# Rows of both attention lanes laid out by dimension in DRAM, and each half of the stacks read back by three transfers

## The reference

```python
x = x + attn_a(layernorm(x))   # memory attention + causal linear attention, 16 heads of 16
x = x + ffn(layernorm(x))      # ternary weights, 256 -> 1024 -> 256, relu
x = x + attn_b(layernorm(x))   # rotary, causal softmax attention, 16 heads of 16
x = x + ffn(layernorm(x))      # the same ffn
```

## Time and profile before

| what | value |
|---|---|
| time, median of 3 runs | 2299.41 us (2298.86 to 2301.97) |
| the profiled execution | 2303.04 us, span 2301.3 us |
| PE (matmul) busy | 1904.0 us, 83% of the span |
| DVE busy | 1617.6 us, 70% |
| ACT busy | 1361.3 us, 59% |
| POOL busy | 1140.6 us, 50% |
| SP's queue: bytes and share of 16 DMA engines | 115.10 MB, 19.8% |
| mean granted TensorE clock | 0.936 |

### The profile page before, as it was taken

How to read it: one execution, slowest core, us unless ns; L and a number is a source line. 1 busy time by engine, 2 the same in 40 slices (tenths; PEclk the granted TensorE clock), 3 DMA queues, 4 the chain that set the end, 5 groups by cost and what they waited for, 6 DMA issues and landing times. The chain is left out here.

```text
span 2301.3 us, 53268 instructions
## 1 busy us (share of the span) xinstructions
PE 1904.0 (83%) x18306; PEld 1207.5 (52%) x18306; DVE 1617.6 (70%) x3890; ACT 1361.3 (59%) x2694; POOL 1140.6 (50%) x978
## 2 busy tenths in 40 slices
PE   0447798989899898989889898989889898988786
PEld 0224455655555555555555555655555555555443
DVE  5546686968777786968777786968777786966351
ACT  0215375666667575666667575666667575665554
POOL 0236347364655547364655547364655547363322
PEclk9757799999999999999999999999999999999998
DMA  3101312304031322303032221304032221303020
GB/s 104 55 10 55 65 57 47 84 5 99 30 70 60 66 66 47 84 9 95 29 70 61 66 66 47 84 2 102 30 65 66 66 66 47 84 2 66 9 58 10
DMA packets 101756, 126.64 MB, mean 55 GB/s; under 512 B 19760, under 2 KB 88496, under 8 KB 97456
## 3 DMA queue, kind: packets, MB, share of 16 engines
q1 hardware_dynamic: 93104, 115.10, 19.8%
q10 hardware_dynamic: 8448, 8.39, 1.1%
HBM read 80.95 MB, written 42.47 MB: 54 GB/s over the span
## 5 line engine op out<-in xcount | busy, mean ns | idle before, releaser
L1268 DVE TENSOR_REDUCE mxs<-bank 128x1 f32<-128x128 f32 (+3 forms) x1024 | 428.0, 482 | 79.7 <-PE bank L1561 78.8
L907 ACT ACTIVATE place<-bank 128x512 f32<-128x512 f32 (+1 forms) x768 | 349.7, 532 | 104.4 <-PE bank L1575 103.1
L669 POOL TENSOR_TENSOR place<-am,place 128x512 f16<-128x512 f32 x256 | 291.0, 1157 | 203.2 <-ACT place L813 203.2
L659 POOL TENSOR_TENSOR place<-place 128x512 f16<-128x512 f32 x256 | 300.7, 1182 | 69.6 <-ACT place L801 64.0
L1559 PE MATMUL bank<-kst,qst 96*128 96x128 f16 (+3 forms) x1024 | 250.8, 306 | 33.5 <-DVE mxs L1268 16.9
L1420 PE MATMUL bank<-w2q,place 128*128 128x256 f16 x2048 | 248.2, 274 | 5.8 <-ACT place L798 4.2
L644 POOL TENSOR_TENSOR rstd<-ve,halfc 128x4 f32<-128x4 f32 x64 | 64.8, 1012 | 364.6 <-DVE ve L1043 364.6
L1573 PE MATMUL bank<-qst,kst 128*128 128x512 f16 (+3 forms) x1024 | 230.7, 302 | 14.6 <-DVE mxs L1268 6.5
L697 POOL TENSOR_TENSOR place<-place 128x512 f16<-128x512 f32 x64 | 83.1, 1301 | 280.9 <-ACT place L837 259.8
L1561 PE MATMUL bank<-mask_qk,identb 128*128 128x128 bf16 x1024 | 218.2, 222 | 0.0
L1420 PEld LDWEIGHTS bank<-w2q,place 128*128 128x128 f16 x2048 | 195.3, 98 | 40.8 <-ACT place L798 11.7
(11 more groups left out here) (162 smaller groups left out, 4134.9 us busy)
## 6 DMA issues: line engine op xcount, KB each, us to landing
by_head<-place SPq DMA_DIRECT2D x64, 256.0 KB, 2.3
qst<-by_head SPq DMA_DIRECT2D x256, 64.0 KB, 2.3
kst<-by_head SPq DMA_DIRECT2D x256, 64.0 KB, 2.3
by_dim<-place SPq DMA_DIRECT2D x64, 256.0 KB, 2.5
kst<-by_dim SPq DMA_DIRECT2D x64, 256.0 KB, 4.7
qst<-by_dim SPq DMA_DIRECT2D x128, 128.0 KB, 5.5
xa<-x SPq DMA_DIRECT2D x16, 512.0 KB, 4.0
out<-xg ACTq DMA_DIRECT2D x16, 512.0 KB, 3.4
```

Of the source, the lines that this page charges most:

```text
L659: G.tensor_tensor(L.hl[:, m, :], L.hf[:, m % 2, :], L.hh[:, m, :], ALU.subtract).then_inc(s["hl"], 1)
L669: G.tensor_tensor(alp[:, n % 2, k, :], am[:, k, :], ahp[:, n % 2, k, :], ALU.subtract).then_inc(s["al"], 1)
L907: A.activation(pf[h % SLOTS][:, S2_COL[k]:S2_COL[k] + S2_W[k]], bank_of(L2, ("S2", h, k))[:, 0:S2_W[k]], ACT.Exp, scale=D ** -0.5 / RS ** ...
L1268: V.tensor_reduce(mxs[:, g:g + 1], bank_of(L2, ("S1", n, k))[:, Q_AT[i]:Q_AT[i] + (i + 1) * P], AX, ALU.max).then_inc(s["mx"], 1)
```

## The change

What a row of the stacks holds is put in another order, so that a whole half can be written to and read from DRAM with few transfers.

- In both lanes the DRAM buffer is now laid out by dimension, then part (high, low), then head. L2's rows already lay by dimension; for L1 the columns of the weights of q and k are permuted at setup (`split_by_dim`), so that row `64r + 4d + i` of a quarter is dimension d of head `4r + i`.
- Each quarter's high and low part is bounced by itself, 128 KB, as soon as it is there: four bounces a half instead of two.
- Each half is read by three transfers: `kst`'s even partitions (high parts, 256 KB), its odd partitions (low parts, 256 KB), and `qst` (512 KB). Each source row is read twice, to two neighbouring partitions, by a repeat of stride 0 that stands second, behind a dimension of 16 rows or more. The bytes are the same as before, 1 MB a half. L1's rows are 4 KB, L2's 8 KB.
- At setup, DVE splits attn_a's q and k weights in 8 strided instructions of 256 elements a partition; `split_by_parity` handles q and k together, with the same 32 instructions of 64 elements as before; the mask that was built on GpSimd (`bd8`) is one reduction on DVE (`bd4`). The chain grows from 66 to 75 links. The 16 small loads of the memories write 16 partitions at a step of 4.
- TensorE's last 16 matmuls of a tile read the same number of columns from other places.

```diff
+                dims, rows = (by_row, P) if L is L1 else (by_dim, PARTS)
+                for which in range(2):
+                    at = 2 * half + which
+                    for part, (name, src) in enumerate((("sh", L.sth), ("sl", L.stl))):
+                        sp.wait_ge(s[name], due(L, name, t, at + 1))
+                        sp.dma_start(dims[half, which, :, part], src[:, at, :]).then_inc(s["bounced"], 16)
+
+                sp.wait_ge(s["bounced"], due(L, "bounced", t, 64 * (half + 1)))
+                stacks = L.qst.shape[1] // KH
+                of_half = slice(half * stacks, (half + 1) * stacks)
+                q_rows = dims[half, 0].rearrange("d a h s -> (d a) (h s)").rearrange("r (o f) -> r o f", o=1)
+                for part in range(2):
+                    k_rows = dims[half, 1, :, part].rearrange("(d o) h s -> d o (h s)", o=1)
+                    sp.dma_start(L.kst[part:rows:2, of_half, :].rearrange("p h s -> p (h s)"),
+                                 k_rows.broadcast_to([rows // 4, 2, stacks * S])).then_inc(L.landed[half], 16)
+                sp.dma_start(L.qst[0:rows, of_half, :].rearrange("p h s -> p (h s)"),
+                             q_rows.broadcast_to([rows // 2, 2, stacks * S])).then_inc(L.landed[half], 16)
...
+            def split_by_dim(mat):
+                stage = w_stage[mat // BQ][:, 0:2 * KH * H].rearrange("p (j i d) -> p j d i", i=QH, d=D)
+                hi, lo = (both(w, mat).rearrange("p (j d i) -> p j d i", i=QH, d=D) for w in (wh, wl))
+                for i in range(QH):
+                    link(V.tensor_scalar(hi[:, :, :, i], stage[:, :, :, i], WS, None, ALU.mult))
+                    link(V.scalar_tensor_tensor(lo[:, :, :, i], stage[:, :, :, i], WS, hi[:, :, :, i],
+                                                ALU.mult, ALU.subtract))
...
-            split_weights(0, BQ)
+            split_by_dim(AQ)
+            split_weights(AV, BQ - AV)
             split_by_parity(BQ)
-            split_by_parity(BK)
...
+            link(V.tensor_reduce(bd4, ident[:, :].rearrange("p (j i) -> p i j", i=QH), AX, ALU.add))
...
-                        ins = T.matmul(local[r][:, i], part[:, n % 2, h % 2, (h // 2) * P:(h // 2 + 1) * P],
+                        ins = T.matmul(local[r][:, i], part[:, n % 2, r, i * P:(i + 1) * P],
```

More of the change, by code:

```diff
@@ L56 @@
 NORM = dict(bn=4, tick=1, mv=4, ve=1, rstd=1, shift=1, xn=4, xt=2, xh=2, xl=2)
-OUTS = dict(v=2, vh=2, sh=4, sl=4, bounced=64, wo=2, xres=2)
+OUTS = dict(v=2, vh=2, sh=4, sl=4, bounced=128, wo=2, xres=2)
 FFN = dict(up=8, hf=8, hh=8, hl=8, xb=1, dn=2, xffn=2)
@@ L69 @@
 PERF = dict(NORM, **FFN, store=16)
-LANDED = {1: 2 * 4 * 2 * 16, 2: 6 * 16}
+LANDED = {1: 3 * 16, 2: 3 * 16}
 CUT = 7
@@ L440, in build @@
         coef = sb("coef", [P, 2, 2, TERMS, QH])
-        bd8 = am[:, 0, 0:HH8]
+        bd4 = am[:, 0, 0:QH]
         t6 = L1.place3[:, 0:3, :].rearrange("p a s -> p (a s)").rearrange("p (r t s) -> p r t s", r=2, t=M + 2)
@@ L455, in build @@
         prec = sb("prec", [P, 2, 16])
-        by_head = nc.dram_tensor("by_head", (KH, 2, P, 2, S), F16, kind="Internal").ap()
-        by_dim = nc.dram_tensor("by_dim", (KH, 2, 2, P, S), F16, kind="Internal").ap()
+        by_row = nc.dram_tensor("by_row", (KH, 2, 2 * D, 2, QH, S), F16, kind="Internal").ap()
+        by_dim = nc.dram_tensor("by_dim", (KH, 2, D, 2, HH8, S), F16, kind="Internal").ap()
         tables = nc.dram_tensor("tables", (2, 2, PAIR, S), F32, kind="Internal").ap()
@@ L474, in build @@
         primed = sem("primed")
-        DVE_SETUP = 66
+        DVE_SETUP = 75
         block = ctx.enter_context(nc.Block())
@@ L519, in _ @@
                 for h in range(HH8):
-                    sp.dma_start(bm[h * D:(h + 1) * D, half, :, h % QH, :], mem[half * HH8 + h]).then_inc(m_in, 16)
+                    r, i = divmod(h, QH)
+                    sp.dma_start(bm[r * PARTS + i:(r + 1) * PARTS:QH, half, :, i, :],
+                                 mem[half * HH8 + h]).then_inc(m_in, 16)
             sp.wait_ge(primed, 1)
@@ L610, in _ @@
             G.memset(mask_kq[:, :], 0.0).then_inc(pool_const, 1)
-            G.memset(bd8, 1.0).then_inc(pool_const, 1)
             G.memset(nt[:, :, :], 0.0).then_inc(pool_const, 1)
             G.memset(halfc[:, :], -0.5).then_inc(pool_const, 1)
-            pool.wait_ge(pool_const, 8)
+            pool.wait_ge(pool_const, 7)
             G.affine_select(out=ident[:, :], in_=ident[:, :], compare_op=ALU.not_equal, fill=1.0, base=0,
@@ L623, in _ @@
                             pattern=[[1, P]], channel_multiplier=-1).then_inc(pool_const, 1)
[L625 to L629, removed]
             pool.wait_ge(c_in, 96)
-            pool.wait_ge(pool_const, 14)
+            pool.wait_ge(pool_const, 11)
             for L in (L1, L2, F2, F1):
@@ L968, in split_weights, with both @@
                 link(V.scalar_tensor_tensor(lo, stage, WS, hi, ALU.mult, ALU.subtract))
-            def split_by_parity(mat):
[L971 to L980, removed]
-            split_weights(0, BQ)
+            def both(tile, mat):
+                return tile[:, mat:mat + 2, :, :].rearrange("p n k f -> p (n k f)")
+            def split_by_dim(mat):
[5 more added lines that the diff above has]
+                                                ALU.mult, ALU.subtract))
+            def split_by_parity(mat):
+                stage = w_stage[mat // BQ][:, 0:2 * KH * H].rearrange("p (j h m r) -> p r m j h", r=2, m=D // 2, h=HH8)
+                hi, lo = (both(w, mat).rearrange("p (j r m h) -> p r m j h", r=2, m=D // 2, h=HH8) for w in (wh, wl))
+                for r in range(2):
+                    for m in range(D // 2):
+                        link(V.tensor_scalar(hi[:, r, m], stage[:, r, m], WS, None, ALU.mult))
+                        link(V.scalar_tensor_tensor(lo[:, r, m], stage[:, r, m], WS, hi[:, r, m], ALU.mult, ALU.subtract))
+            split_by_dim(AQ)
+            split_weights(AV, BQ - AV)
             split_by_parity(BQ)
-            split_by_parity(BK)
             split_weights(BV, NMAT - BV)
@@ L1006, in _ @@
                 link(V.scalar_tensor_tensor(w, stage, small[:, 4 + n:5 + n], below, ALU.is_gt, ALU.subtract))
-            dve.wait_ge(pool_const, 14)
+            dve.wait_ge(pool_const, 11)
             link(V.tensor_copy(identh[:, :], ident[:, :]))
+            link(V.tensor_reduce(bd4, ident[:, :].rearrange("p (j i) -> p i j", i=QH), AX, ALU.add))
             link(V.tensor_copy(identb[:, :], ident[:, :]))
@@ L1026, in _ @@
                                    bm[rows, :, :, :, D].rearrange("p a m h -> p (a m) h")))
-                link(V.tensor_copy(bdmask[rows, :, :], bd8[rows, heads].rearrange("p (h o) -> p h o", o=1)
+                link(V.tensor_copy(bdmask[rows, :, :], bd4[rows, :].rearrange("p (h o) -> p h o", o=1)
                                    .broadcast_to([PARTS, QH, VW])))
```

## The result

The changed kernel took 2329.19 us at the median of 4 runs (2324.48 to 2331.94), the kernel before 2300.69 of 4 (2298.86 to 2303.91): ratio 1.0119, 95% interval 1.0107 to 1.0131. It is slower by 28.5 us, where 2.3 us less were forecast, and outside the range that was given. The profiled execution took 2329.01 us with a span of 2327.3; before, the span was 2301.3. The mean granted clock is 0.938 against 0.936, so the clock is not the cause. 26.0 us of span are to be explained.

The account below looks back on a forecast made before the run. Iterations were taken to follow the clock and the engines' fixed orders, with only 11.4 us of PE's stack waits removable. Terms +2.5 - 1.8 - 2.1 - 0.9 = -2.3 us took the median from 2299.4 to 2297.1, range 2290.5 to 2303.5.

Parts of the forecast that it names:

- the setup step: DVE's setup chain: more strided splits and a reduction cost +2.5 us, up to +3.5 with some instruction fetch.
- The loop's term: Later iterations: five PE waits of 3.9 us for L2's rows go, ACT's relu gives some back; -0.9 us.
- The rival "setup costs more": Setup costs +3.5 us and little is kept elsewhere: +0.9, with a late pace 2304 to 2306; chance 0.08.
- Sequence 0 in L1: L1's first rows land earlier, then DVE's own work limits when it takes the product; -1.8 us.
- Sequence 0 in L2: L2's first rows land 2.9 us earlier, but DVE then waits for xa; -2.1 us kept.
- the slow stretch of 131 GB/s: In L2's old read, the later, slower window, ascribed to reads to 16 partitions; 303 GB/s in the other.
- the rival of the changed pace: Loop iterations without the wait take the later, slower pace: 1.6 us lost, about 3 more by clock, 2302; chance 0.17.
- forecast of no change: Whole kernel: -2.3 us, 0.1%, below the 0.2% (4.6 us) a measurement can tell; chance 0.60.
- Slow repeated reads: Rival: stack reads with repeated rows are slow; at twice the present 8.6 us, 100 us lost, 2400; chance 0.05.
- The clock's gain: Rival: PE's new timing makes the short low-clock stretch the rule, ten iterations by 1.3 us: 2284; chance 0.06.
- The waits were not carried in full: Rival: all PE's stack waits become time saved, 11.4 us removed, 2.5 added, 2290.5; chance 0.14.

Follow-up runs that it names:

- Experiment 1: The kernel before with nine tiny memsets added at the head of DVE's setup, nothing else changed: 2333.02 us against 2301.34, ratio 1.0133.
- experiment 2: The changed kernel with 120 tiny memsets added at the head of DVE's setup: 2301.62 us, ratio 1.0006 to the kernel before.
- experiment 5: The changed kernel with merged weight splits (43 links instead of 75) plus 23 tiny memsets ahead: 2295.97 us against 2302.10 for the kernel before, ratio 0.9973.

## Why the prediction was wrong

**The step that failed** is the setup step's last clause: the nine added links were counted for the work that they do, plus "some instruction fetch" once. Their effect on the loop, which no longer lies as it did in DVE's program, was not counted, and DVE's return to its head was not named as a cost at all. The loop's term was -0.9 us and measured +26.0, the whole difference of the spans. Experiment 1 (nine idle links, the same loss) and experiment 2 (the stall alone gone, the same time as before) show that this is the stall: 24.5 us by the changed kernel with and without it. None of the five rivals was of this kind. The rival "setup costs more" came nearest in its cause and was priced at up to 2306.

The other terms are small against what one execution differs from the next. There are 14 profiles, of the two kernels and the 12 experiments, so those that have a piece of the change can be put beside those that don't.

**Setup** cost more than the +2.5 forecast. The first layernorm begins at 70.90 instead of 66.23, where 68.7 was to be seen. 0.86 us of this is the weights landing later, which is chance: DVE's first split starts between 20.2 and 24.1 over the 14 profiles. The change itself costs +3.8. Of it 3.4 is the splits, mostly the strided pairs, which no row had shown:

```profile
22.78 0.45 DVE L962 TENSOR_SCALAR wh<-qst 128x256 f16<-128x256 f32 x1 [17.98 <-DMA kst<-wall]
23.27 0.73 DVE L963 SCALAR_TENSOR_TENSOR wl<-qst,wh 128x256 f16<-128x256 f32 x1
...
27.78 0.69 DVE L952 TENSOR_SCALAR wh<-qst 128x1024 f16<-128x1024 f32 x1
```

Four pairs take 27.78 - 22.78 = 5.0 us against 3.8 forecast. The first operation was about right (0.45 for 0.41), the second was not, 0.73 for 0.46: (0.73 - 0.26)/192 = 2.4 ns for each element beyond the row of 64, where the 1.04 ns of the contiguous rows had been taken. The reduction took 0.38 us for 0.25.

**Sequence 0 in L1** was right. DVE takes the product as soon as its own work ends:

```profile
99.36 0.40 PE L1431 MATMUL bank<-qst,kst 64*128 64x128 f16 x8 [0.78 <-DVE place L1204]
100.24 0.74 DVE L1154 TENSOR_TENSOR winv<-wrec,wsum 128x32 f32<-128x32 f32 x2
101.01 1.29 DVE L1095 SCALAR_TENSOR_TENSOR am<-bank,tri 128x512 f32<-128x512 f32 x2
```

101.01 against 98.26 in the earlier trace rows is +2.75, of which setup is +4.67: 1.9 us gained, 1.8 forecast, and limited by DVE's own chain, as said. From the first layernorm to this product it is 29.6 to 30.1 us in the four profiles with the change in L1, and 30.8 to 32.3 in the ten without; the means differ by 1.8.

**Sequence 0 in L2** was right in mechanism and less in size. The read is faster by less than was forecast, and DVE then waits for xa, as forecast:

```profile
264.29 1.19 SPq L545 DMA_DIRECT2D kst<-by_dim  x2
265.52 0.59 SPq L547 DMA_DIRECT2D qst<-by_dim  x1
...
271.72 0.23 PE L1552 MATMUL bank<-kst,qst 96*128 96x128 f16 x1 [2.44 <-DMA qst<-by_dim]
274.43 1.40 DVE L1029 BATCH_NORM_STATS2 stats<-xa 128x6 f32<-128x256 f32 x4 [0.47 <-DMA xa<-x]
```

From the first issue to PE's matmul it is 7.4 us, 8.6 before; the forecast had 5.5 to 7. In the five profiles with the new read it is 7.3 to 7.6 us, in the nine without it 8.6 to 9.6. The term itself can be read from xa's issue to DVE's layernorm: 274.43 - 270.04 = 4.39 us against 5.68, so 1.3 us were kept and not 2.1. Over the profiles it is 4.2 to 4.4 against 5.5 to 6.7, 1.7 by the means. The prediction let xa land 3.6 us behind its issue, where the earlier trace rows had 4.0. The interval to the next xa is no measure of it: 128.24 became 126.38, but in the nine profiles without the new read it varies from 126.8 to 128.6 by itself.

An estimate from the rate on the page "SBUF — State Buffer" of the Trainium skill, section "Door 1: the DMA port swizzle", would have been 5.3 us for this read. The trace doesn't bear it out here: the 7.4 us are longer, though they include some 1.8 us of issuing. The prediction also gave the slow stretch of 131 GB/s to the reads to 16 partitions; a window counts all transfers in flight together, so that is not shown.

**The loop without the stall** was right in mechanism, and its size can't be told. No wait for a stack is left in it, and PE's L1413 waits for ACT in its place:

```profile
533.20 1.27 PE L1413 MATMUL bank<-w2q,place 128*128 128x256 f16 x10 [0.40 <-ACT place L783]
```

From the first scores to L1613 every iteration takes 12.7 us (529.96 to 542.63 in this one), as forecast. Between the marks of xa the changed kernel with 120 links takes 1556.4 us and the two other kernels with the new read and no stall 1556.4 and 1556.5. The kernel before takes 1554.9, and with 4 and with 7 links, also without a stall, 1556.5 and 1559.3. So neither the 0.9 us gained nor the 1.6 lost of the rival of the changed pace can be told from nothing.

**The sum without the stall.** By the means above it is 3.8 - 1.8 - 1.7 + 0 = +0.3 us; the run without the stall measured +0.06% (+0.3 us) with an interval from -1.4 to +3.9. For experiment 5 it is -2.1 - 1.8 - 1.7 = -5.6 us, and -6.1 were measured. The agreement is closer than terms from a few profiles deserve. So the forecast of no change was right for the change's work and wrong for the program that it makes. Its size, -2.3 us, was missed even there, by setup, L2 and the loop, and is too small for the runs to tell.

**The rivals.** Slow repeated reads are refuted: 512 KB took 4.7 us to 128 partitions and 6.3 to 64, at the median. The clock's gain isn't there (0.938 for 0.936). The waits were not carried in full: that rival's 11.4 us less 3.8 of setup would have shown in experiment 2.

## What to carry to other kernels

An engine's loop has a place in its program, and a few instructions more or less ahead of it or in it can turn a free return into a stall of some 3 us an iteration, as DVE's did here. So look in the table of waits for "issue" at the first instruction of each loop and at the packets of the instruction queues before any edit that changes an instruction count, and compare them after it. Where a small edit costs more than the work that it adds, add idle instructions ahead of the loop, where the engine waits anyway, and measure at several numbers of them before the edit itself is blamed.

## What was not expected of the hardware

- DVE's return to its loop head costs at most 0.2 us or 2.6 to 2.9 us (3.7 to 4.0 in one kernel), by the place of its body in blocks of 128 instructions. A body of 375 is free at about eight places of 128. A head at a block's end costs a second stall of 1.1 to 2.1 us.
- Only a fifth to a quarter of such a stall was hidden here: 2.0 to 2.2 us of 2.75 reached the iteration of the changed kernel, since PE waits for DVE right behind it.
- Writing f16 with a stride, the two-input operation of 256 elements a partition took 0.73 us and the one-input operation 0.45; on 1024 contiguous elements they took 1.22 and 0.69.
- Reading each row twice by a repeat in the second dimension was not slow: 1 MB in three transfers was in use 7.4 us after the first issue, against 8.6 to 9.6 for the six transfers without a repeat.
